# Two selective-scan phases: delta of the next unit first, and GpSimd takes a tile of every other state in the second

## The reference, cut to what matters

```
delta = softplus(dts + bias)                  # dts = W_dt @ (W_x @ u)[:rank]
h[n]  = exp(delta * A[n]) * h[n] + delta * u * B[n]      # n = 0..15, one step per position
y     = sum_n h[n] * C[n] + D * u
```

## Time and profile before

| | us |
|---|---|
| median of 3 runs | 31563.71 |
| lowest and highest | 31561.78, 31573.28 |
| the profiled execution | 31560.8 |
| its span, first to last instruction | 31559.0 |
| mean granted clock of TensorE | 0.966 of full speed |
| busy PE, PEld | 25016.3, 9492.8 |
| busy DVE, ACT, POOL | 26869.6, 16242.0, 24325.1 |

### The profile page before, as it was taken

How to read it: one execution, slowest core, us unless ns; L and a number is a source line. 1 busy time by engine, 2 the same in 40 slices (tenths; PEclk the granted TensorE clock), 3 DMA queues, 4 the chain that set the end, 5 groups by cost and what they waited for, 6 DMA issues and landing times. The chain is left out here.

```text
span 31559.0 us, 218343 instructions
## 1 busy us (share of the span) xinstructions
PE 25016.3 (79%) x57532; PEld 9492.8 (30%) x57532; DVE 26869.6 (85%) x22560; ACT 16242.0 (51%) x26679; POOL 24325.1 (77%) x10344
## 2 busy tenths in 40 slices
PE   8777777777777777777777777766999888888877
PEld 3222222222222222222222222222333322222222
DVE  9899999999999999999999999964111399999984
ACT  2455555555555555555555555532222355555552
POOL 1799999999999999999999999951000266666652
PEclk9999999999999999999999999988999999999998
DMA  6433333333333333333333333355111244444456
GB/s 205 170 134 133 130 134 133 134 133 131 135 132 134 133 132 134 132 133 133 133 134 131 133 132 134 133 178 201 61 51 51 102 165 166 166 166 166 166 174 192
DMA packets 1142621, 4396.74 MB, mean 139 GB/s; under 512 B 247888, under 2 KB 285792, under 8 KB 776032
## 3 DMA queue, kind: packets, MB, share of 16 engines
q1 hardware_dynamic: 1035472, 4033.56, 34.6%
q10 hardware_dynamic: 105904, 349.22, 3.2%
HBM read 3715.33 MB, written 667.03 MB: 139 GB/s over the span
## 5 line engine op out<-in xcount | busy, mean ns | idle before, releaser
L856 DVE TENSOR_TENSOR_SCAN s_h<-s_dA,s_state,s_dbu 128x512 f32<-128x512 f32 x15296 | 18659.9, 1267 | 626.5 <-ACT s_dA L721 621.9
L794 POOL TENSOR_TENSOR s_dbu<-s_du,s_b_sb 128x1536 f32<-128x1536 f32 (+1 forms) x5634 | 17656.0, 3135 | 1467.0 <-DVE s_h L856 1441.0
L721 ACT ACTIVATE s_dA<-s_delta,s_negA 128x512 f32<-128x512 f32 x15360 | 10323.0, 685 | 6070.8 <-DVE s_h L856 6055.9
L596 PE MATMUL s_y_ps<-s_hc,s_ident 128*128 128x512 f32 x22528 | 10813.0, 602 | 0.6 <-DVE s_hc L866 0.5
L866 DVE TENSOR_TENSOR s_hc<-s_h,s_c_ps 128x1024 f32<-128x1024 f32 x5632 | 6737.1, 1196 | 238.1 <-issue 218.6
L586 PE MATMUL s_c_ps<-s_bc,s_sel 96*128 96x512 bf16 x7168 | 2553.9, 391 | 4952.7 <-DVE s_hc L866 4949.9
L596 PEld LDWEIGHTS s_y_ps<-s_hc,s_ident 128*128 128x128 f32 x22528 | 4386.9, 195 | 3497.7 <-issue 3190.9
L803 POOL TENSOR_TENSOR s_hc_pool<-s_h,s_c_sb 128x512 f32<-128x512 f32 x4096 | 5161.2, 1260 | 1.4 <-DVE s_h L856 1.3
L604 PE MATMUL s_y_ps<-s_hc_pool,s_ident 128*128 128x512 f32 x8192 | 4229.2, 598 | 0.0
L811 POOL TENSOR_TENSOR s_du<-s_delta,s_u 128x1536 f32<-128x1536 f32 (+1 forms) x450 | 1125.0, 2500 | 3350.4 <-ACT s_delta L708 3299.6
L586 PEld LDWEIGHTS s_c_ps<-s_bc,s_sel 96*128 96x128 bf16 x7168 | 575.1, 97 | 8696.9 <-DVE s_hc L866 8161.9
(11 more groups left out here) (131 smaller groups left out, 15106.4 us busy)
## 6 DMA issues: line engine op xcount, KB each, us to landing
s_b_sb<-rows SPq DMA_DIRECT2D x1794, 1024.0 KB, 4.7
s_c_sb<-rows SPq DMA_DIRECT2D x1024, 1024.0 KB, 6.2
s_u<-U SPq DMA_DIRECT2D x257, 768.0 KB
Y<-s_yo ACTq DMA_DIRECT2D x256, 768.0 KB, 3.3
m_y<-Y SPq DMA_DIRECT2D x192, 1024.0 KB, 7.5
s_u<-U SPq DMA_DIRECT2D x193, 256.0 KB
U<-f_row SPq DMA_DIRECT2D x24, 2048.0 KB, 17.3
U<-f_col SPq DMA_DIRECT2D x24, 2048.0 KB, 7.1
```

The costliest lines, as they stand in the source:

```text
L596: last = pe.matmul(y_ps[:, t, :], ident[:, :], hc[:, s % 2, j, :], start=False, stop=s == NS - 1 and j // nd == ng - 1)
L721: act.activation(dA[:, n % DECAYS, :], delta[g % 2][:, t, :], ACT.Exp, scale=negA[g % 2][:, a:a + 1]).then_inc(dA_ready, 1)
L794: pool.tensor_tensor(dbu[:, s % AHEAD, :, :], a, b, ALU.mult).then_inc(dbu_ready, 1)
L856: dve.tensor_tensor_scan(h[:, s % (2 * GROUP), j, :], dA[:, (n * J + j) % DECAYS, :], dbu[:, s % AHEAD, j, :], initial, ALU.mult, ALU.add) ...
```

## The change

It touches scan_phase alone. `at` is replaced by a table for each of the three engines.

- Order of preparation, both phases: xproj, then dt and softplus, then the two rests. TensorE does dt at states 3, 4, 5 and rests at 8 and 10 in s0 (before: rests at 3, 4, dt at 5, 6, 7); in s1 dt at 2 and rests at 4 and 5 (before: rests at 2, 3, dt at 4). ScalarE does, in s0, softplus at 7 (8), scale_ident at 8 (10), rests at 9 and 11 (3, 4), evacuate_pool at 4 (3), store at 6 (5); in s1 evacuate at 2 (1), take_xproj at 2 (1), softplus at 4 (5), store at 4 (3), scale_ident at 5 (6), rests at 6 and 7 (2, 3). GpSimd does take_du at 11 (13) in s0, still at 7 in s1. Waits change with it: xproj waits for the rests of the unit before instead of its delta, rest waits for delta, dt for the copies of xproj alone.
- In s1 SHARE becomes (0, 2, 4, 6): the second tile of these states is multiplied by C on GpSimd, TensorE broadcasts one row of C for them instead of two, and sums that tile from s_hc_pool. One broadcast of C a unit, 1 MB, is added to SyncE's queue between store_rows and the first B of the next unit. evacuate waits for these sums too.

```diff
--- before.py
+++ after.py
@@ -368,7 +368,7 @@
     GROUPS = NS // GROUP
     DECAYS = 3 if nd > 1 else 4
 
-    SHARE = tuple(range(NS)) if nd > 1 else ()
+    SHARE = tuple(range(NS)) if nd > 1 else (0, 2, 4, 6)
     NSH = len(SHARE)
     LAG = 3 if nd > 1 else 2
 
@@ -376,11 +376,14 @@
     STEPS_IN = ROWS_IN // ng
     PARTS_IN = NS // STEPS_IN
     C_PARTS = NSH // ROWS_IN
-    C_STEP = ng
-
-    at = (dict(xproj=0, take=2, mid=3, low=4, dt=(5, 6, 7), soft=8, scale_ident=10, du=13, evacuate_pool=3, store=5)
-          if nd > 1 else
-          dict(xproj=0, take=1, mid=2, low=3, dt=(4,), soft=5, scale_ident=6, du=7, store=3))
+    C_STEP = ng * (SHARE[1] - SHARE[0])
+
+    on_pe = (dict(xproj=0, dt=(3, 4, 5), mid=8, low=10) if nd > 1 else
+             dict(xproj=0, dt=(2,), mid=4, low=5))
+    on_act = (dict(evacuate=1, take=2, evacuate_pool=4, dt=(4, 5, 6), store=6, soft=7, scale_ident=8, mid=9, low=11)
+              if nd > 1 else
+              dict(evacuate=2, take=2, soft=4, store=4, scale_ident=5, mid=6, low=7))
+    on_pool = dict(du=11 if nd > 1 else 7)
 
     def in_product(s):
         return J - 1 if s in SHARE else J
@@ -514,8 +517,7 @@
             store_rows(0)
             broadcast_b(0, 0)
             broadcast_b(0, 1)
-            if nd > 1:
-                broadcast_c(0, 0)
+            broadcast_c(0, 0)
             for g in range(units):
                 load(g + 1)
                 if nd > 1:
@@ -533,6 +535,8 @@
                     broadcast_b(g, 2)
                     broadcast_b(g, 3)
                     store_rows(g + 1)
+                    if g + 1 < units:
+                        broadcast_c(g + 1, 0)
                     broadcast_b(g + 1, 0)
                     if g + 1 < units:
                         broadcast_b(g + 1, 1)
@@ -546,7 +550,7 @@
 
                 q = g % 2
                 pe.wait_ge(loaded[q], loads_of(g))
-                wait(pe, delta_ready, g)
+                wait(pe, bc_ready, g * 3)
                 for t in range(nd):
                     last = pe.matmul(prep_ps[0:XROWS + rank], wx[q][:, t, :], u[q][:, t, :],
                                      start=t == 0, stop=t == nd - 1)
@@ -555,13 +559,15 @@
             def rest(g, part):
 
                 pe.wait_ge(bc_ready, g * 3 + 1 + part)
+                pe.wait_ge(delta_ready, g + 1)
                 pe.matmul(prep_ps[0:64, :], twice[:, :], xd[0:32, :], start=True, stop=False)
                 pe.matmul(prep_ps[0:64, :], minus[:, part, :], bc16[g % 2][:, :],
                           start=False, stop=True).then_inc(rest_done, 1)
 
             def dt(g, t):
 
-                pe.wait_ge(bc_ready, g * 3 + 3)
+                pe.wait_ge(xd_ready, g + 1)
+                pe.wait_ge(bc_ready, g * 3 + 1)
                 if t:
                     pe.wait_ge(dt_read, g * nd + t)
                 pe.matmul(prep_ps[:, :], wdt[g % 2][XROWS:XROWS + rank, t, :], xd[XROWS:XROWS + rank, :],
@@ -594,7 +600,7 @@
                 for j in range(in_product(s)):
                     t = j % nd
                     last = pe.matmul(y_ps[:, t, :], ident[:, :], hc[:, s % 2, j, :],
-                                     start=False, stop=s == NS - 1 and j // nd == ng - 1)
+                                     start=False, stop=nd > 1 and s == NS - 1)
                 last.then_inc(summed, 1)
 
             def pool_sum(g, s):
@@ -606,15 +612,14 @@
 
             def unit(g):
                 for s in range(NS):
-                    if s == at["xproj"]:
+                    if s == on_pe["xproj"]:
                         xproj(g + 1)
-                    if s == at["mid"]:
+                    if s in on_pe["dt"]:
+                        dt(g + 1, on_pe["dt"].index(s))
+                    if s == on_pe["mid"]:
                         rest(g + 1, 0)
-                    if s == at["low"]:
+                    if s == on_pe["low"]:
                         rest(g + 1, 1)
-                    for t in range(nd):
-                        if s == at["dt"][t]:
-                            dt(g + 1, t)
                     c_broadcast(g, s)
                     if s == 1:
                         direct(g, range(OWN), evacuated)
@@ -633,10 +638,10 @@
             pe.wait_ge(sel_ready, 1)
             pe.wait_ge(minus_set, 2)
             xproj(0)
+            for t in range(nd):
+                dt(0, t)
             for part in range(2):
                 rest(0, part)
-            for t in range(nd):
-                dt(0, t)
             for g in range(units):
                 unit(g)
             state_sum(units - 1, NS - 1)
@@ -681,6 +686,8 @@
 
                 q = g % 2
                 act.wait_ge(summed, (g + 1) * NS)
+                if nd == 1:
+                    act.wait_ge(summed_pool, (g + 1) * NSH)
                 wait(act, stored[q], 16 * (g // 2))
                 act.activation(yo[q][:, 0:OWN, :], y_ps[:, 0:OWN, :], ACT.Copy).then_inc(evacuated, 1)
 
@@ -742,34 +749,34 @@
                         save_states(g, s // GROUP - 1)
                     for j in range(J):
                         decay(g, s, j)
-                    if s == 1 and g:
+                    if s == on_act["evacuate"] and g:
                         evacuate(g - 1)
-                    if nd > 1 and s == at["evacuate_pool"] and g:
+                    if nd > 1 and s == on_act["evacuate_pool"] and g:
                         evacuate_pool(g - 1)
-                    if s == at["take"]:
+                    if s == on_act["take"]:
                         take_xproj(g + 1)
-                    if s == at["mid"]:
+                    if nd > 1 and s in on_act["dt"]:
+                        take_dt(g + 1, on_act["dt"].index(s))
+                    if s == on_act["soft"]:
+                        softplus(g + 1)
+                    if s == on_act["scale_ident"]:
+                        scale_ident(g + 1)
+                    if s == on_act["mid"]:
                         take_rest(g + 1, 0)
-                    if s == at["low"]:
+                    if s == on_act["low"]:
                         take_rest(g + 1, 1)
-                    if nd > 1 and s in at["dt"]:
-                        take_dt(g + 1, at["dt"].index(s))
-                    if s == at["scale_ident"]:
-                        scale_ident(g + 1)
-                    if s == at["soft"]:
-                        softplus(g + 1)
-                    if s == at["store"] and g:
+                    if s == on_act["store"] and g:
                         store(g - 1)
 
             act.wait_ge(sel_ready, 1)
             take_xproj(0)
-            for part in range(2):
-                take_rest(0, part)
             if nd > 1:
                 for t in range(nd):
                     take_dt(0, t)
             softplus(0)
             scale_ident(0)
+            for part in range(2):
+                take_rest(0, part)
             for g in range(units):
                 unit(g)
             save_states(units - 1, GROUPS - 1)
@@ -817,7 +824,7 @@
                     elif s < AHEAD and g and NS + s - AHEAD in SHARE:
                         times_c(g - 1, NS + s - AHEAD)
                     input_of(g + s // NS, s % NS)
-                    if s == at["du"]:
+                    if s == on_pool["du"]:
                         take_du(g + 1)
 
             take_du(0)
@@ -848,7 +855,7 @@
 
                     if n >= 2 * GROUP:
                         dve.wait_ge(hc_ready, n - 2 * GROUP + 1)
-                        wait(dve, hcp_ready, pool_products_to(n - 2 * GROUP))
+                        dve.wait_ge(hcp_ready, pool_products_to(n - 2 * GROUP))
                     if s % GROUP == 0:
                         wait(dve, state_saved, g * GROUPS + s // GROUP - 1)
                 dve.wait_ge(dA_ready, n * J + j + 1)
```

## The result

| | median us | ratio to before, 95% interval |
|---|---|---|
| before | 31562.7 (4 runs) | |
| after | 31380.6 (4 runs, 31364.5 to 31409.6) | 0.9943 (0.9926 to 0.996) |

A forecast was written before the change was run, and what follows sets the result against it. GpSimd was taken to bound the first phase, VectorE's work plus two waits for dA the second. 192 x (2.12 + 1.25) + 5 = 652 us off 31560.8 gave 30909, stated as 30910; range 30860 to 31155.

The forecast's parts named there:

- What bounds each phase: First phase: GpSimd alone, 77.3 us a unit; second: VectorE's own work and two waits for dA, 29.29 us a unit.
- rival 4: Second phase: no idle time left, state 5 on time, 25.68 us a unit, 30863 us; at the edge of the forecast's 0.62.
- (a): Second phase, VectorE: four products with C a unit cover 512 instead of 1024, saving 0.53 us each, 2.12 us a unit.
- (b): Second phase, GpSimd: takes four products, 4.9 us a unit; its 24.7 us fit into 25.9, despite the skill's advice.
- (c): Second phase, TensorE: four fewer broadcasts of C, some 23 us a unit, not the bound; 0.2 us left for state 5.
- (d): Second phase, ScalarE's new order: both waits for dA go, up to 1.45 us a unit, 1.25 counted.
- (e): Second phase: delta comes earlier, so GpSimd's wait of 1.57 us for it goes; no gain of its own.
- (f): Second phase, SyncE's queue and DMA: with C added, B lands at about 14.4 us, wanted at 16.1; cost nothing.
- (g): First phase: same steps in another order, GpSimd without a gap, unit still 77.3 us; cost 0, gain excluded.
- (h): Start of each phase: two rests come off the way to the first delta, 2.7 us, twice, 5 us.
- rival 2: Second phase: GpSimd becomes the bound, or TensorE at state 5; 30987 to 31025 us; chance 0.17.
- Rival 1: Second phase: waits for dA only change place, 27.17 us a unit, 31154 us, or 31090 without small pieces; chance 0.15.

The follow-up runs named there:

- e6: Changed kernel with the four shared rows of C put side by side by permuting weight columns and selection matrix, results right: 30871 us.
- e3: Changed kernel with SHARE empty and no broadcast of C in the second phase, the new order of preparation alone: 31283 us.
- e5: Kernel before with the sharing alone (SHARE, broadcast of C, evacuate's wait for GpSimd's sums), old order of preparation: 31751 us.
- e1: Changed kernel with the second phase's broadcast of C behind load in SyncE's queue, not ahead of the next unit's first B: 30902 us.
- e10: e5 with one more edit: in the second phase evacuate stands behind the decays of state 2 instead of state 1: 31438 us.

## Why the prediction was wrong, point by point

- **What bounds each phase**: right. First phase 77.3 us a unit before and after, GpSimd without a gap; in the second VectorE's own work is the floor (e6: 25.73 us, rival 4 had 25.68).
- **(a)** right: 0.54 us a product; e3 to e6 give 27.85 - 25.73 = 2.12 us a unit.
- **(b)** right: with B on time GpSimd is busy 3745.8 of 3900 us (e6), 24.7 of 25.73 us. The Trainium skill's advice against it, cited there, did not decide the sign: with B on time the sharing wins 2.12 us a unit, and e5 loses by VectorE's waits for ScalarE and not by GpSimd's work.
- **(c)** right: no wait at state 5 shows in e6, so the 0.2 us kept back for it was not needed.
- **(d)** right, under-sized: 1.44 us a unit (e3), not 1.25.
- **(e)** right: no wait for delta is left.
- **(f)** wrong, and it is the step that failed. "Nothing" was 2.6 us a unit, 500 us. The count starts, as in the prediction, with the old unit's last product; in the unit shown that is

```profile
27022.90 1.20 DVE L873 TENSOR_TENSOR s_hc<-s_h,s_c_ps 128x1024 f32<-128x1024 f32 x1
```

B lands at 27047.56 - 27022.90 = 24.7 and not at 14.4, with GpSimd ready at 21.1. Three terms fell. C's landing: I took a C for "equally large" as a B and so equally dear, 2.8 us. It holds its queue for 5 to 7 us, as an estimate: 7 by the landings (9.7, against 4.7 to 5.0 for contiguous rows that take 2.1), 4.9 by the DMA shares of e1 and e3 (0.73 x 25.82 - 0.50 x 27.85). The landing of the rows: left out of the sum, although C and B read what is stored and wait for it. It is 1.6 us at best and 4.3 in the unit shown, where a B stands just ahead. So even in e6, with a cheap C, B lands at 16.3 us, 1 us before GpSimd wants it, and my margin of 1.7 us against 14.4 was counted too wide. The issue of the rows: 27030.53 - 27022.90 = 7.6, where e6 has 5.9, because ScalarE's copy ends only then:

```profile
27029.93 0.57 ACT L668 ACTIVATE s_xd<-s_prep_ps 100x512 f32<-100x512 f32 x1
```

It is late by what TensorE does, told under the rivals below. I also gave the step one answer and no bounds. The trace before had some in its first phase, 10000 to 15000 us, where C's four rows lie side by side. Its landing there, and then that of the rows:

```profile
DMA to landing us min/median/max: 4.2/6.2/10.2
```

```profile
rows<-s_xd SPq DMA_DIRECT2D x64, 64.0 KB, 4.0
```

- **(g)** right: cost 0. **(h)** was too small to be told.
- **The rivals**: rival 2 had "GpSimd becomes the bound" at 31000, by its work plus the old wait for delta. It did become the bound, by a wait on DMA, at 28.3 us. Rival 1 did not come in the full change, but is what e5 shows. The side effect on TensorE was in no rival. The load stands behind the late B's in SyncE's queue, TensorE waits 383.2 / 141 = 2.7 us a unit for it, and then a sum runs at half the clock; TensorE in the unit shown:

```profile
27022.93 1.10 PE L555 MATMUL s_prep_ps<-s_u,s_wx 128*100 128x512 f32 x2 [3.05 <-DMA s_keep_in<-in_keep]
...
27024.46 3.58 PE L602 MATMUL s_y_ps<-s_hc,s_ident 128*128 128x512 f32 x4
```

3.58 us for a sum that took 1.88, behind an idle stretch of 3.05 us. The granted clock from 27024.5 to 27028.0 is 0.51, the lower of the two levels; over that phase it fell from 1.00 to 0.94, and is 1.00 in e6. This sum is what ScalarE's evacuation and with it the copy of the rows wait for, so it is part of the loop. A bound on (f) would have held the time, as an estimate: with 4.0 us for the rows and 10.2 for C, B lands at 6.5 + 4.0 + 10.2 + 2.8 = 23.5, 7.4 us after GpSimd wants it, and a unit takes up to 24.7 + 7.4 = 32.1 us.

## What to carry to other kernels

When an edit frees a bound engine by handing work to another, the transfers that feed the new work are part of the price: follow each in its queue, with what stands ahead of it and behind it, and give a transfer whose form isn't in the trace a bound and not the price of its neighbour. When two halves of a change are measured apart, a half can lose (e5), and a loss can hide another (e10). When an engine waits for a transfer whose issue waits for that engine, look for a loop: here the late engine made its own next input later still. And when any one of three small edits regains everything, each of them was about as large as the wait: that alone does not tell which link to blame.

## What the runs showed of the hardware that I had not expected

One DMA of 1 MB from four rows of 2 KB to 128 partitions lands in 5.0 us with the rows side by side, 6.2 with 4 KB from row to row, and 9.7 with 8 KB. 64 KB that stand 0.5 us behind 1 MB in the same queue land in 4.7 us instead of 1.6.
